# A local attention's band mask: from products on TensorE to one add-and-max on VectorE and selects on GpSimd

## Chip, cores, metric

The kernel runs on one core of a Trainium2 chip. The metric is its device time in microseconds (us), the median of several executions.

## The reference

Two decoder layers for 16 batch entries of 256 tokens and 256 features, all in fp32. The change is in the second block of the first layer, a cross attention in a local window:

```python
q, k, v = heads(x @ Wq + bq), heads(ctx @ Wk + bk), heads(ctx @ Wv + bv)   # 16 heads of 16 features
scores = einsum("bhqd,bhkd->bhqk", q, k) / sqrt(16)
scores = where(abs(i - j) <= 64, scores, masked)                           # a band: 64 keys to each side
x = layernorm(x + softmax(scores) @ v @ Wo + bo)
```

Around it stand a linear attention with a feed-forward network, a chain of six attention cells ("c" below, full 256 by 256 scores), a causal linear attention, a second cross attention with a padding mask ("y" below) and a Fourier layer. They are not changed.

## The kernel before

Every entry goes through the same list of some 500 steps. A step is a short piece of work on one engine: a product, a transposition, an eviction of a PSUM bank, a reduction. Four entries are under way at a time, each with its own buffers, and a fifth starts when the first is done. `program_plan` runs over all steps of all entries with a cost in us for each, as written in `entry_steps` (`do(engine, op, a, us, needs...)`), and picks for every engine, whenever it is free, a ready step, by entry and by the length of what hangs on it, with a little noise from `SEEDS`. What comes out are fixed lists, `PLAN["PE"]`, `PLAN["DVE"]`, `PLAN["ACT"]`, `PLAN["POOL"]` and `PLAN["SP"]`: each engine works through its own list in order and waits on semaphores where something is not there yet. So a step that takes longer than its cost says holds up what stands behind it on its engine, whatever the entry. PSUM has eight banks, and the plan assigns them too.

The attention works on quads: eight heads go in one step, four groups of 32 partitions with two heads in each, one of the two zeroed in the keys. The local attention has four such steps per entry, n = 0 to 3, kind "x", hence 64 in the kernel. One of them goes like this:

- `s` on TensorE (`tensor`, op "s"): the scores, queries on the partitions, four banks, each with two runs of 192 columns (`SPAN`), since a block of 128 queries sees at most 192 keys. Before, `banded` first writes the band into each bank (a product of `ident_bf` with `band`, 2 x 192 columns of 0 or -1e30 in bf16), and the score products add to it.
- `s` on VectorE, once for each pair p of banks: the maxima over the keys, negated, into `nmx`.
- `split` on VectorE: the maxima as three bf16 parts. `nm` on TensorE transposes them, and ScalarE copies them into SBUF.
- `st` on TensorE: the same scores again, transposed (keys on the partitions). Before, `banded` comes first here too; then the score products, and a product of `ones_bf` with the negated maxima that subtracts them.
- `exp` on ScalarE, for each pair p: exponentials from PSUM to `work` in SBUF, two banks of 2 x 192 columns each.
- `pv` on TensorE: the exponentials times the values. The row sums come with it, then `part`, `sums` and `norm`.

The quads of kinds "c" and "y" go the same way with 256 columns and without a band. GpSimd's list holds mostly the elementwise products of the first attention ("mix1" and "mix2", 16 of each per entry, `L1631` and `L1641`).

Of the kernel before, what the change touches and what calls it, by code (L numbers as in the profile page):

```python
# [72 lines left out]
SEEDS = (981929, 264616, 376881, 660340, 622402, 125658, 701981, 998496, 712956, 113630)  # L73
# [73 lines left out]
def entry_steps():  # L147
# [59 lines left out]
    def heads(n, q, k, v):  # L207
        kind, c, f, par = quad(n)
        b = do("PE", "s", n, 0.88 if kind != "x" else 1.4, q, k, *((nm_done[n - 2],) if n >= 2 else ()),
               takes=("score", "score"))  # L210
        maxed = [do("DVE", "s", (n, p), 1.13 if kind != "x" else 0.87, b, frees=((b, p),)) for p in range(2)]
# [4 lines left out]
        s = st_done[n] = do("PE", "st", n, 1.12 if kind != "x" else 1.6, nm,   # L216
# [3 lines left out]
        both = (do("DVE", "add", n, 1.2, *e),) if kind == "c" else ()  # L220
        pv = do("PE", "pv", n, 1.3 if kind == "c" else 0.9, *e, *both, v,
# [245 lines left out]
class Dry:  # L467
# [7 lines left out]
    affine_select = dma_start = stream_shuffle = wait_ge = then_inc = drain = _self  # L475
# [9 lines left out]
def build(nc, x, ctx_in, mask, w_all, w_setup, cols, rows, ew, act_w, out):  # L485
    ctx = ExitStack()
    with ctx:
# [22 lines left out]
        ones_bf = sb("ones_bf", [P, P], BF16)  # L510
        ewb = sb("ewb", [P, 3 * NODES])
# [178 lines left out]
        def tensor(e):  # L690
# [61 lines left out]
            def banded(b, count):  # L752
                for j in range(count):
                    e.matmul(b[j // 2][j % 2].rearrange("p (c n) -> p c n", c=NC)[:, :, 0:SPAN], ident_bf[:, :],  # L754
                             band[:, :, :], start=True, stop=False)

# [10 lines left out]
            for i, op, a, units in PLAN["PE"]:  # L767
# [106 lines left out]
                elif op == "s":  # L874
# [12 lines left out]
                    if kind == "x":  # L887
                        banded(b, 4)
                    for cc in range(NC):
                        kk = queries(kind, cc)  # L890
                        for g in range(4):
                            ins = e.matmul(b[g // 2][g % 2][:, cc * 256:cc * 256 + kk.stop - kk.start],  # L892
                                           q[32 * g:32 * g + 32, f, cc * P:cc * P + P],
                                           k[32 * g:32 * g + 32, f, kk], start=(kind != "x"),
                                           stop=(kind != "x" or cc == NC - 1), tile_position=(32 * g, 0))
# [9 lines left out]
                elif op == "st":  # L905
# [4 lines left out]
                    if kind == "x":  # L910
                        banded(b, 4)
                    e.wait_ge(*when("nm", a, i))
                    for kc in range(NC):
                        qq = queries(kind, kc)
                        o = slice(kc * 256, kc * 256 + qq.stop - qq.start)
                        for g in range(4):
                            e.matmul(b[g // 2][g % 2][:, o], k[32 * g:32 * g + 32, f, kc * P:kc * P + P],  # L917
                                     q[32 * g:32 * g + 32, f, qq], start=(kind != "x"), stop=False,
                                     tile_position=(32 * g, 0))
                        for g in range(4):  # L920
                            ins = e.matmul(b[g // 2][g % 2][:, o], ones_bf[32 * g:32 * g + 3, :],  # L921
# [892 lines left out]
```

## Time and profile before

| | |
|---|---|
| median of 3 runs | 3567.08 us (3566.13 to 3568.82) |
| profiled execution, own time | 3568.07 us |
| its span | 3566.3 us |
| granted TensorE clock, mean | 0.964 of full speed |
| TensorE busy | 3242.3 us, 91% |
| VectorE busy | 2329.9 us, 65% |
| ScalarE busy | 1695.1 us, 48% |
| GpSimd busy | 1019.1 us, 29% |

The span is the stretch from the first to the last instruction that the profiler recorded; the time of the execution is 1.8 us longer. Busy is the union of an engine's instructions, so time in which two of them overlap counts once.

### The profile page before, as it was taken

The numbers are of one execution on the slowest core, as the hardware profiler recorded it, in microseconds if no ns is written. First come the engines' busy times: TensorE is split into PE (matmuls) and PEld (weight loads), VectorE is DVE, ScalarE is ACT, GpSimd is POOL, SyncE is SP. The second block draws the span as 40 slices with busy tenths as digits, with TensorE's granted clock in tenths as the row PEclk, the third lists the DMA queues.
The fourth block names the chain that finished last, engine by engine and source line by source line (L and its number), as shares of the span: only waits on it lengthen the run. The fifth ranks groups of instructions, "written<-read, shape, count | busy, mean of one in ns | idle before, by whom it ended". The sixth has DMA issues, their size and how long they took to land.

```text
span 3566.3 us, 77500 instructions
## 1 busy us (share of the span) xinstructions
PE 3242.3 (91%) x31372; PEld 2395.2 (67%) x31372; DVE 2329.9 (65%) x4137; ACT 1695.1 (48%) x3472; POOL 1019.1 (29%) x795
## 2 busy tenths in 40 slices
PE   7899999998999999899999999999899999999876
PEld 6777767676766667676666766667676666766644
DVE  6675658667676766767577675766767676464533
ACT  1244454544545455444635445354454545554532
POOL 7872006042331413333041332304233141000000
PEclk8999999999999999999999999999999999999986
DMA  6210011010101101010100101101010110100000
GB/s 207 89 45 31 19 29 39 29 40 19 46 19 40 31 23 46 16 41 26 37 28 25 43 19 37 31 29 39 19 46 19 40 31 16 37 14 10 13 7 4
DMA packets 123276, 122.88 MB, mean 34 GB/s; under 512 B 9776, under 2 KB 122672, under 8 KB 122800
## 3 DMA queue, kind: packets, MB, share of 16 engines
q1 hardware_dynamic: 122928, 117.91, 10.9%
q8 instruction: 258, 4.23, 0.5%
q14 instruction: 90, 0.74, 0.1%
HBM read 113.69 MB, written 4.19 MB: 33 GB/s over the span
## 4 chain that ended last, share of the span: by engine, by line
PE 60%; DVE 15%; ACT 9%; issue 8%; POOL 7%; DMA 1%; SPq 0%; DVEq 0%; POOLq 0%; ACTq 0%
PE banks L747 16%; PE banks L739 11%; PE banks L892 7%; PE banks L917 6%; DVE nmx L1251 5%; PE banks L945 5%; POOL work L1641 3%; ACT work L1482 3%; PE banks L732 2%; PE banks L754 2%; PE banks L855 2%; PE banks L903 2%; POOL work L1631 2%; PE banks L952 1%; PE banks L921 1%
## 5 line engine op out<-in xcount | busy, mean ns | idle before, releaser
L747 PE MATMUL banks<-work,weights 128*128 128x256 f32 x3584 | 868.3, 390 | 56.4 <-DVE work L1275 51.5
L1251 DVE TENSOR_REDUCE nmx<-banks 128x4 f32<-128x1024 f32 (+3 forms) x684 | 725.4, 1099 | 250.5 <-PE banks L892 248.7
L747 PEld LDWEIGHTS banks<-work,weights 128*128 128x128 f32 x3584 | 678.3, 194 | 189.0 <-DVE work L1275 53.9
L1482 ACT ACTIVATE work<-banks 128x1024 f32<-128x1024 f32 (+3 forms) x679 | 595.1, 937 | 288.7 <-PE banks L921 288.7
L739 PE MATMUL banks<-weights,work 128*128 128x256 f32 x2688 | 653.7, 389 | 20.7 <-ACT work L1482 4.4
L739 PEld LDWEIGHTS banks<-weights,work 128*128 128x128 f32 x2688 | 499.3, 193 | 124.9 <-issue 39.7
L1641 POOL TENSOR_TENSOR work<-work 128x512 f32<-128x512 f32 x256 | 407.3, 1615 | 366.4 <-DVE work L1221 216.9
L892 PE MATMUL banks<-work 32*128 32x256 f32 (+1 forms) x5120 | 357.5, 394 | 60.5 <-DVE nmx L1251 27.2
L917 PE MATMUL banks<-work 32*128 32x256 f32 (+1 forms) x5120 | 391.4, 394 | 18.0 <-DVE nmx L1251 6.8
L1631 POOL TENSOR_TENSOR work<-work 128x512 f32<-128x512 f32 x256 | 346.6, 1375 | 148.7 <-DVE work L1217 134.7
L1269 DVE TENSOR_TENSOR added<-work 128x1024 f32<-128x1024 f32 x192 | 281.3, 1469 | 129.3 <-ACT work L1482 118.7
L945 PE MATMUL banks<-work 128*32 128x256 f32 (+3 forms) x5632 | 341.2, 364 | 5.3 <-ACT work L1482 4.6
L1675 POOL TENSOR_TENSOR work<-work,row 128x512 f32<-128x512 f32 x64 | 91.9, 1437 | 888.0 <-PE banks L732 888.0
L892 PEld LDWEIGHTS banks<-work 32*128 32x128 f32 x5120 | 234.6, 187 | 157.2 <-issue 125.7
L917 PEld LDWEIGHTS banks<-work 32*128 32x128 f32 x5120 | 214.0, 190 | 132.1 <-issue 81.2
L945 PEld LDWEIGHTS banks<-work 128*32 128x32 f32 x5632 | 158.3, 111 | 148.4 <-issue 82.4
L1384 ACT ACTIVATE work<-banks,cb 128x256 f32<-128x256 f32 x384 | 161.4, 475 | 149.2 <-PE banks L747 149.2
L1221 DVE TENSOR_REDUCE work<-work 128x32 f32<-128x512 f32 x256 | 173.2, 678 | 86.2 <-POOL work L1641 85.7
L1466 ACT ACTIVATE work<-banks 128x256 f32<-128x256 f32 x320 | 119.2, 385 | 212.7 <-PE banks L903 212.3
L1217 DVE TENSOR_REDUCE work<-work 128x32 f32<-128x512 f32 x256 | 171.6, 679 | 69.7 <-POOL work L1631 68.1
L921 PE MATMUL banks<-work,ones_bf 3*128 3x256 bf16 (+1 forms) x2560 | 190.8, 272 | 0.0
L732 PE MATMUL banks<-ident,work 128*128 128x128 f32 x768 | 122.1, 285 | 67.0 <-DVE work L1201 47.6
(156 smaller groups left out, 3525.2 us busy)
## 6 DMA issues: line engine op xcount, KB each, us to landing
weights<-in_w_all SPq DMA_DIRECT2D x322, 256.0 KB, 2.8
work<-in_w_setup SPq DMA_DIRECT2D x41, 256.0 KB, 5.1
work<-in_ctx SPq DMA_DIRECT2D x32, 256.0 KB, 3.1
work<-in_x SPq DMA_DIRECT2D x16, 256.0 KB, 3.0
out<-work SPq DMA_DIRECT2D x16, 256.0 KB, 2.2
weights<-in_w_all SPq DMA_DIRECT2D x1, 3072.0 KB, 15.0
row<-in_rows SPq DMA_DIRECT2D x1, 1280.0 KB, 9.2
mrow<-in_mask SPq DMA_DIRECT2D x16, 32.0 KB, 3.2
```

The costliest lines, as they stand in the source:

```text
L732: ins = e.transpose(b[:, f * 256 + c * P:f * 256 + c * P + P], src[:, c, f * P:f * P + P], ident[:, :])
L739: ins = e.matmul(b[:, m * 256:m * 256 + 256], xin[:, k, m * P:m * P + P], wslot(w)[:, k, :], start=(k == 0 and (m == 0 or closed)) if star ...
L747: ins = e.matmul(b[:, m * 256:m * 256 + 256], wslot(w)[:, k, m * P:m * P + P], xin[:, k, :], start=(k == 0 and (m == 0 or closed)) if star ...
L892: ins = e.matmul(b[g // 2][g % 2][:, cc * 256:cc * 256 + kk.stop - kk.start], q[32 * g:32 * g + 32, f, cc * P:cc * P + P], k[32 * g:32 * g ...
L917: e.matmul(b[g // 2][g % 2][:, o], k[32 * g:32 * g + 32, f, kc * P:kc * P + P], q[32 * g:32 * g + 32, f, qq], start=(kind != "x"), stop=False,
L921: ins = e.matmul(b[g // 2][g % 2][:, o], ones_bf[32 * g:32 * g + 3, :], upper(stored_nmax(s, a))[32 * g:32 * g + 3, qq], start=False, stop ...
L945: ins = e.matmul(b[32 * g:32 * g + 32, lo:hi], left, right[:, kc * 256 + lo - qq.start:kc * 256 + hi - qq.start], start=(kc == 0), stop=(k ...
L1251: ins = e.tensor_reduce(nmax(s, n)[:, 2 * p + j:2 * p + end, :], b.rearrange("p j (c n) -> p j c n", c=NC)[:, :, :, 0:w], AX, ALU.max, neg ...
L1269: e.tensor_tensor(added[:, half], pt(half, 0, 4)[:, :, 0:S], pt(half, 0, 4)[:, :, S:2 * S], ALU.add).then_inc(*tell(vec[s], "added", a, i))
L1482: ins = e.activation(dst, b.rearrange("p j (c n) -> p j c n", c=NC)[:, :, :, 0:w], ACT.Exp)
L1631: e.tensor_tensor(big1, q.unsqueeze(2).broadcast_to([P, PH, NH, DH]), k.unsqueeze(1).broadcast_to([P, PH, NH, DH]), ALU.mult).then_inc(*te ...
L1641: e.tensor_tensor(big2, mix.unsqueeze(2).broadcast_to([P, PH, DH, NH]), v.unsqueeze(1).broadcast_to([P, PH, DH, NH]), ALU.mult).then_inc(* ...
```

## The change

In the local attention the band leaves TensorE. `banded` is gone from `s` and `st`. The maxima are taken by four VectorE instructions for each pair of banks, one for each bank and block of queries: each adds the band to 192 columns of scores in PSUM, writes the sum back there, and gives the maximum of the sums as its accumulator output. These maxima are not negated, so `st` subtracts them with a constant of -1 (`minus_bf`). The transposed scores have no band any more; ScalarE takes exponentials of all 192 columns, and a new GpSimd step, `band`, then sets those outside the band to zero with four selects for each pair. `pv` waits for it. The plan's costs and its `SEEDS` are changed as well, so all the lists are made anew.

```diff
-SEEDS = (981929, 264616, 376881, 660340, 622402, 125658, 701981, 998496, 712956, 113630)
+SEEDS = (271952, 450768, 66414, 843758, 204716)
...
-        b = do("PE", "s", n, 0.88 if kind != "x" else 1.4, q, k, *((nm_done[n - 2],) if n >= 2 else ()),
+        b = do("PE", "s", n, 0.88, q, k, *((nm_done[n - 2],) if n >= 2 else ()),
                takes=("score", "score"))
-        maxed = [do("DVE", "s", (n, p), 1.13 if kind != "x" else 0.87, b, frees=((b, p),)) for p in range(2)]
+        maxed = [do("DVE", "s", (n, p), 1.13, b, frees=((b, p),)) for p in range(2)]
...
-        s = st_done[n] = do("PE", "st", n, 1.12 if kind != "x" else 1.6, nm, 
+        s = st_done[n] = do("PE", "st", n, 1.12 if kind != "x" else 1.0, nm, 
...
+        if kind == "x":
+            e = [do("POOL", "band", (n, p), 1.0, e[p]) for p in range(2)]
         pv = do("PE", "pv", n, 1.3 if kind == "c" else 0.9, *e, *both, v,
...
-            def banded(b, count):
-                for j in range(count):
-                    e.matmul(b[j // 2][j % 2].rearrange("p (c n) -> p c n", c=NC)[:, :, 0:SPAN], ident_bf[:, :],
-                             band[:, :, :], start=True, stop=False)
...
                     b = [take("score", "max", a, 0, i), take("score", "max", a, 1, i)]
-                    if kind == "x":
-                        banded(b, 4)
...
                     book(i, a)
-                    if kind == "x":
-                        banded(b, 4)
                     e.wait_ge(*when("nm", a, i))
+                    added_row = minus_bf if kind == "x" else ones_bf
...
+                        if kind == "x" and kc == 0:
+                            e.wait_ge(*when("band", a, 0, i))
+                            e.wait_ge(*when("band", a, 1, i))
...
                     w = SPAN if kind == "x" else S
+                    if kind == "x":
+                        for j in range(2):
+                            b = at("max", n, p, i)[j]
+                            for c in range(NC):
+                                ins = e.tensor_tensor_reduce(out=b[:, c * 256:c * 256 + SPAN], in0=b[:, c * 256:c * 256 + SPAN], in1=band[:, c, :],
+                                                             scale=1.0, scalar=3 * MASKED, op0=ALU.add, op1=ALU.max,
+                                                             accum_out=small[s]["nmx"][:, n % 2, c, 32 * (2 * p + j):32 * (2 * p + j) + 1])
+                        ins.then_inc(*freed("max", n, p, i))
+                        continue
...
+                elif op == "band":
+                    n, p = a
+                    e.wait_ge(*when("exp", n, p, i))
+                    both = pt(half_of.get((i, n), 0), 2 * p, 2)
+                    for lo, hi, base, sign in ((0, WINDOW, WINDOW, 1), (WINDOW, SPAN, 0, -1), (256, 256 + P, 0, 1),
+                                               (256 + P, 256 + SPAN, 0, -1)):
+                        part = both[:, :, lo:hi]
+                        ins = e.affine_select(out=part, in_=part, compare_op=ALU.is_ge, fill=0.0, base=base,
+                                              pattern=[[0, 2], [sign, hi - lo]], channel_multiplier=-sign)
+                    ins.then_inc(*tell(pool[s], "band", n, p, i))
```

TensorE's list, in the middle of the program, at a place where a quad of the local attention is scored (`s`) and the first one of the same entry is exponentiated (`st`). Before, each row of score products (`L892`, `L917`) has the four band products (`L754`) ahead of it:

```order
L754 MATMUL banks<-band,ident_bf 128x2x192 x4
L892 MATMUL banks<-work 128x192 x8
L739 MATMUL banks<-weights,work 128x256 x4
L747 MATMUL banks<-work,weights 128x256 x4
L903 MATMUL banks<-ident,nmx 128x128 x2
L754 MATMUL banks<-band,ident_bf 128x2x192 x4
L917 MATMUL banks<-work 128x192 x4
L921 MATMUL banks<-work,ones_bf 128x192 x4
```

Now, at the corresponding place (`L888` scores, `L898` the transposition of the maxima, `L911` and `L915` the transposed scores and the subtraction, `L942` the products with the values, all other rows products and transpositions of other steps):

```order
L888 MATMUL banks<-work 128x192 x8
L742 MATMUL banks<-weights,work 128x256 x4
L735 MATMUL banks<-ident,work 128x128 x4
L750 MATMUL banks<-work,weights 128x256 x4
L911 MATMUL banks<-work 128x192 x4
L915 MATMUL banks<-work,minus_bf 128x192 x4
L911 MATMUL banks<-work 128x192 x4
L915 MATMUL banks<-work,minus_bf 128x192 x4
L888 MATMUL banks<-work 128x256 x8
L750 MATMUL banks<-work,weights 128x256 x4
L888 MATMUL banks<-work 128x256 x8
L898 MATMUL banks<-ident,nmx 128x128 x4
```

The band products are gone. Behind the last of these rows comes the `pv` of the same quad, so 4 rows of other work (two of scores, one of four products, one of four transpositions) stand between `st` and `pv`.

VectorE's list. Before, the maxima of the first quads of an entry in the local attention (`L1251`) and their split (`L1257`, `L1260`):

```order
L1251 TENSOR_REDUCE nmx<-banks 128x2x2
L1257 TENSOR_TENSOR nmx<-nmx 128x4x2
L1260 TENSOR_TENSOR nmx<-nmx 128x4x2
L1251 TENSOR_REDUCE nmx<-banks 128x2 x2
L1221 TENSOR_REDUCE work<-work 128x32
```

Now, the last of the eight pairs of rows that one quad has, and what comes behind:

```order
L1251 ISA banks,nmx<-banks,band 128x192
L1251 ISA nmx 128x1
L1341 TENSOR_TENSOR work<-work,banks 128x512
L1363 SCALAR_TENSOR_TENSOR work<-banks,ykw,work 128x512 x2
L1175 BN_STATS st<-work 128x6 x2
L1179 BN_AGGR mv<-st 128x2 x2
L1263 TENSOR_TENSOR nmx<-nmx 128x4x2
L1266 TENSOR_TENSOR nmx<-nmx 128x4x2
```

Where one row took the maxima of two banks, eight rows stand now: for each bank and block of queries the add-and-max, and behind it a second instruction that writes out the accumulator.

GpSimd's list, where the next entry's products `mix1` (`L1638`) go on; the selects are `L1658`:

```order
L1629 TENSOR_SCALAR work<-work 128x512 x2
L1638 TENSOR_TENSOR work<-work 128x512 x8
L1658 AFFINE_SELECT work<-work 128x2x64
L1658 AFFINE_SELECT work<-work 128x2x128 x2
L1658 AFFINE_SELECT work<-work 128x2x64 x2
L1658 AFFINE_SELECT work<-work 128x2x128 x2
L1658 AFFINE_SELECT work<-work 128x2x64
L1638 TENSOR_TENSOR work<-work 128x512 x2
```

Eight selects for a quad are new, inside the run of products; before, that run was not interrupted by the local attention. Of the four quads of this entry two stand in this run, and two in a quieter stretch ahead of it.

## Rows read from the trace of the kernel before

**Rows 1.** The page's first part: busy time of each engine.

```profile
PE 3242.3 (91%) x31372; PEld 2395.2 (67%) x31372; DVE 2329.9 (65%) x4137; ACT 1695.1 (48%) x3472; POOL 1019.1 (29%) x795
```

**Rows 2.** The chain that ended last: shares by engine, shares by line.

```profile
PE 60%; DVE 15%; ACT 9%; issue 8%; POOL 7%; DMA 1%; SPq 0%; DVEq 0%; POOLq 0%; ACTq 0%
...
by line: PE banks L747 16.2%; PE banks L739 11.3%; issue 8.3%; PE banks L892 6.6%; PE banks L917 5.8%; DVE nmx L1251 5.4%; PE banks L945 4.8%; POOL work L1641 3.4%; ACT work L1482 3.2%; PE banks L732 2.2%; PE banks L754 2.1%; PE banks L855
```

**Rows 3.** One entry's period in mid-run: stretch, length, busy (instructions), clock.

```profile
1637.00:1849.00 212.00, 196.10 (x1945) 144.03 (x1938) 146.01 (x256) 105.41 (x217) 63.42 (x48) 0.98 0.11 32
```

**Rows 4.** Groups by form, PE: busy us, mean ns; idle before, releasers.

```profile
L754 PE MATMUL banks<-band,ident_bf 128*128 128x384 bf16 x512 | 111.1, 342 | 16.7 <-DVE nmx L1251 13.4 <-ACT work L1482 1.6 <-DVE work L1287 1.1
```

**Rows 5.** Timeline of PE, an `st` and an `s`: start us, us, line.

```profile
1732.08 0.81 PE L754 MATMUL banks<-band,ident_bf 128*128 128x384 bf16 x4 [1.10 <-DVE nmx L1251]
1732.82 0.61 PE L917 MATMUL banks<-work 32*128 32x192 f32 x8
...
1748.33 0.82 PE L754 MATMUL banks<-band,ident_bf 128*128 128x384 bf16 x4
1749.08 0.93 PE L892 MATMUL banks<-work 32*128 32x192 f32 x16
```

**Rows 6.** The page's group of L1251, then DVE groups by form.

```profile
L1251 DVE TENSOR_REDUCE nmx<-banks 128x4 f32<-128x1024 f32 (+3 forms) x684 | 725.4, 1099 | 250.5 <-PE banks L892 248.7
...
L1251 DVE TENSOR_REDUCE nmx<-banks 128x4 f32<-128x768 f32 x114 | 105.2, 949 | 33.0 <-PE banks L892 32.7
L1275 DVE TENSOR_TENSOR work<-banks,work 128x256 f32<-128x256 f32 x192 | 80.5, 419 | 116.6 <-ACT work L1497 116.3
L1329 DVE TENSOR_TENSOR work<-banks,causal 128x512 f32<-128x512 f32 x128 | 78.2, 678 | 3.8 <-PE banks L1024 3.8
L1285 DVE SCALAR_TENSOR_TENSOR work<-banks,em,work 128x256 f32<-128x256 f32 x64 | 30.8, 481 | 231.6 <-PE banks L945 231.6
L1170 DVE RECIPROCAL kept<-kept 128x1 f32<-128x1 f32 x16 | 2.6, 164 | 0.6
```

**Rows 7.** Timeline of DVE: start to start of back-to-back instructions.

```profile
1660.42 0.96 DVE L1251 TENSOR_REDUCE nmx<-banks 128x4 f32<-128x768 f32 x1 [1.97 <-PE banks L892]
1661.29 0.17 DVE L1257 TENSOR_TENSOR nmx<-nmx 128x8 f32<-128x8 f32 x1
...
1745.49 0.25 DVE L1182 BATCH_NORM_AGGREGATE mv<-st 128x2 f32<-128x6 f32 x2
```

**Rows 8.** Timeline of POOL: the selects that build the constants.

```profile
4.33 0.30 POOL L1581 TENSOR_SCALAR_AFFINE_SELECT ident<-ident 128x128 f32<-128x128 f32 x1 [0.23 <-POOL eps L1578]
4.58 0.30 POOL L1581 TENSOR_SCALAR_AFFINE_SELECT ident_bf<-ident_bf 128x128 bf16<-128x128 bf16 x1
...
5.11 0.52 POOL L1586 TENSOR_SCALAR_AFFINE_SELECT band<-band 128x384 bf16<-128x384 bf16 x1
5.58 0.29 POOL L1588 TENSOR_SCALAR_AFFINE_SELECT causal<-causal 128x128 bf16<-128x128 bf16 x1
```

**Rows 9.** Two DVE lines (min/median/max ns), and a stretch with GpSimd beside.

```profile
L1269 DVE TENSOR_TENSOR added<-work x192: 1210/1226/2286, 233.9 to 3463.2; 128x1024 f32<-128x1024 f32 x192
L1275 DVE TENSOR_TENSOR work<-banks,work x192: 391/423/426, 239.1 to 3468.7; 128x256 f32<-128x256 f32 x192
...
1740.37 1.27 POOL L1675 TENSOR_TENSOR work<-work,row 128x512 f32<-128x512 f32 x1 [28.43 <-PE banks L732]
1740.52 2.20 DVE L1269 TENSOR_TENSOR added<-work 128x1024 f32<-128x1024 f32 x1 [1.26 <-ACT work L1482]
```

**Rows 10.** Who waited for whom: us in total, times, longest us.

```profile
PEld banks L903 <- DVE nmx L1260: 42.2, 22, 4.6
PE banks L903 <- DVE nmx L1260: 35.7, 16, 4.2
```

**Rows 11.** Timeline behind that `st`: its exponentials, the next `pv`.

```profile
1733.98 1.57 ACT L1482 ACTIVATE work<-banks 128x768 f32<-128x768 f32 x3 [2.27 <-PE banks L921]
...
1736.25 0.90 PE L945 MATMUL banks<-work 128*32 128x192 f32 x24
```

More of the change, by code:

```diff
@@ L474 @@
     scalar_tensor_tensor = tensor_reduce = reciprocal = tensor_copy = bn_stats = bn_aggr = memset = _self
-    affine_select = dma_start = stream_shuffle = wait_ge = then_inc = drain = _self
+    tensor_tensor_reduce = affine_select = dma_start = stream_shuffle = wait_ge = then_inc = drain = _self
 class Signal:
@@ L510, in build @@
         ones_bf = sb("ones_bf", [P, P], BF16)
+        minus_bf = sb("minus_bf", [P, P], BF16)
         ewb = sb("ewb", [P, 3 * NODES])
@@ L893, in tensor @@
                                            q[32 * g:32 * g + 32, f, cc * P:cc * P + P],
-                                           k[32 * g:32 * g + 32, f, kk], start=(kind != "x"),
-                                           stop=(kind != "x" or cc == NC - 1), tile_position=(32 * g, 0))
+                                           k[32 * g:32 * g + 32, f, kk], start=True, stop=True, tile_position=(32 * g, 0))
                             if cc == NC - 1 and g == 1:
@@ L917, in tensor @@
                             e.matmul(b[g // 2][g % 2][:, o], k[32 * g:32 * g + 32, f, kc * P:kc * P + P],
-                                     q[32 * g:32 * g + 32, f, qq], start=(kind != "x"), stop=False,
+                                     q[32 * g:32 * g + 32, f, qq], start=True, stop=False,
                                      tile_position=(32 * g, 0))
                         for g in range(4):
-                            ins = e.matmul(b[g // 2][g % 2][:, o], ones_bf[32 * g:32 * g + 3, :],
+                            ins = e.matmul(b[g // 2][g % 2][:, o], added_row[32 * g:32 * g + 3, :],
                                            upper(stored_nmax(s, a))[32 * g:32 * g + 3, qq], start=False,
-                                           stop=(kind != "x" or kc == NC - 1), tile_position=(32 * g, 0))
+                                           stop=True, tile_position=(32 * g, 0))
                             if kc == NC - 1 and g == 1:
@@ L1571, in gpsimd @@
             e.memset(ones_bf[:, :], 1.0)
+            e.memset(minus_bf[:, :], -1.0)
             e.memset(mark[:, :, :], 0.0)
```

## The prediction

> **What bounds the kernel now.** I read the page's first part, then the chain, then one period in mid-run, then the places where the change works. TensorE is busy 91% of the span, VectorE 65%, GpSimd 29% [rows 1]. A stretch of 212 us in mid-run, one entry's period, says the same: TensorE 196.1 us, VectorE 146.0, GpSimd 63.4, at a granted clock of 0.98 [rows 3]. The chain that ended last lies 60% on TensorE, 15% on VectorE, 7% on GpSimd [rows 2]. So TensorE is the bound, but not alone: 9% of the span (324 us) it has nothing running, and the longest waits that I name below are for VectorE. Four entries interleave, and each engine's list is fixed. So an edit counts by how much of it lies on that chain, and I use the chain's shares as exchange rates.
>
> **What it takes off TensorE.** 64 quads have a set of four band products ahead of `s` and another ahead of `st`: 512 products, 128 sets. Together they are busy 111.1 us [rows 4]. The start of a set to the start of the score products behind it is 1749.08 - 1748.33 = 0.75 us for an `s` and 0.74 for an `st` [rows 5]; the set reads 0.82 busy because its end overlaps what follows. So 128 x 0.75 = 96 us of issue time go, and that is the most that this part can give. Of these products 2.1% of the span, 75 us, lies on the chain [rows 2]; with the overlap taken out, 75 x 0.75 / 0.82 = 68 us. I take -68. The score products and the subtraction keep their counts and columns: 0.
>
> **What it puts on VectorE.** A pair of banks had one reduction over 768 columns, 949 ns long, the next instruction starting 0.87 us after it [rows 6, 7]. Where the two banks are not neighbours it was split in two. 128 pairs now have four add-and-max instructions of 192 columns and four that write out the accumulator. Neither stands in the trace. The first reads PSUM and one tensor in SBUF, as two lines do that take 419 ns for 256 columns and 678 for 512: 1.01 ns a column, so 354 ns for 192 [rows 6]. Instructions that follow each other start about 0.08 us before the last one ends (0.949 against 0.87), so 0.27 from start to start. The second instruction writes one column; two tiny ones in a row take 0.25 us together, each some 0.15 to 0.17 long, so about 0.10 from start to start [rows 6, 7]. Lower bound of a couple: 0.27 + 0.07 (a start 0.08 ahead of the end of the shortest) = 0.34. Upper bound: neither overlaps, 0.354 + 0.164 = 0.52, and 0.06 more if it decodes like the line with a per-partition scalar, which takes 481 where the plain one takes 419 [rows 6]: 0.58. I take 0.40: all the operands are constants, and every VectorE row that I looked at overlaps its successor, with something added because the second needs the first's sum. So 4 x 0.40 = 1.60 for a pair instead of 0.87, and 128 x 0.73 = 94 us more on VectorE. Of line L1251's 725 us, all attentions together [rows 6], the chain holds 5.4% of the span, 193 us, or 27% [rows 2]; 0.27 x 94 = +25.
>
> The plan reckons 1.13 us for such a pair, less than my 1.60, so behind each pair the VectorE list runs 0.5 us late against the plan. What stands there is the split, which TensorE's transposition of the maxima waits for (42.2 and 35.7 us in total before) [rows 10], and other entries' evictions. The 27% covers this as long as the lateness is a few us a quad.
>
> **What it puts on GpSimd.** Two selects of 128 columns start 0.25 us apart, one of 384 is followed after 0.47 [rows 8]: 0.86 ns a column and 0.14 fixed. A pair has two selects of 2 x 64 and two of 2 x 128 columns: 2 x 0.25 + 2 x 0.36 = 1.22 us. These were bf16 or fp32 constants, and the new ones are fp32 with two levels; the nearest rows for the other end are GpSimd's ordinary operations (1.27 us for 512 columns) [rows 9], 2.5 ns a column, which would make it 768 x 2.5 = 1.9 us. 128 x 1.22 = 156 us on 1019, 33% of the span. What hides it: in the list of TensorE four rows of other work stand between an `st` and its `pv`, 44 instructions as the trace counts them, at the period's pace (196.1 / 1945 = 0.10 us) 4.4 us. Needed are the exponentials, which take 1.57 us for both pairs [rows 11], the first pair done after some 0.8, then 2 x 1.22: 3.3 us. So it fits by 1 us at that place, and if GpSimd is in the middle of a product of 1.3 us it just doesn't. Inside the run of products `mix1` the selects wait for the exponentials, and the products behind them wait too; those belong to an entry that has just begun. I take +4.
>
> With the selects comes some contention. The add with two inputs in SBUF takes 1226 ns in the median and up to 2286; the row that took 2.20 us began 0.15 us after GpSimd began one of 1.27, and ended about one normal duration after GpSimd did. The line with one input in PSUM never exceeds 426 ns [rows 9]. The new add-and-max is of the second sort, so GpSimd doesn't hold it. The selects can hold the first sort, for at most 0.25 to 0.36 us, 4% of the time: within the +4. The Trainium skill, *SBUF — State Buffer*, Who interferes with whom, says that a VectorE instruction with two SBUF inputs shares an interface with GpSimd's reads and the later one is blocked; the trace agrees.
>
> **The sum.** From the profiled execution's own time, 3568: -68 + 25 + 4 = -39, so 3529, and with the order new everywhere no finer than 3530. The profiled execution is 1 us above the median of the runs, so no correction. 0.2% is 7 us, about what a measurement of this kernel can tell from no change.
>
> **Rivals.**
>
> - *The gain in full* (0.14). The new VectorE work falls into its idle 35%, and only issue time on TensorE counts: 3568 - 96 = 3472, to 3505 with a third of it lost. For it: the period has 66 us of VectorE idle per entry and needs 6 more. Against it: VectorE already stands on 15% of the chain, and `s`, maxima, split, `nm` and `st` of a quad are one chain.
> - *The add-and-max is dear, and VectorE takes over in the local attention* (0.23); this one ends on the other side. At 0.58 a pair takes 2.32, 186 us more than before. A quad then holds VectorE 4.6 us in a piece, against the 2.3 that the plan reckons, and all other entries' evictions, transposed maxima and layer norms wait behind it. The part above my 94 us, 92 us, then counts nearly in full: 3529 + 92 = 3621 at the most, 3590 with two thirds. It decides from the price at which the excess eats the 39 us: at the full rate 39 / 512 = 0.08 above 0.40, so slower from about 0.48 us a couple. The Trainium skill has a rule for this case: *VectorE: DVE Perf Modes*, The DRAIN you can't avoid, says that the next operation does not start until the pipe is empty, and another section of that page that an accumulator output makes two instructions. The order shows the two instructions; the starts 0.08 us ahead of the end speak against the first rule. What it would give here, worked out from the durations: 0.354 + 0.164 = 0.52 a couple, 61 us above my sum at the full rate, 3590, and 3545 at the 27%.
> - *GpSimd comes late* (0.07). At 1.9 us a pair, `pv` needs 0.8 + 3.8 = 4.6 us where 4.4 are covered, and 2 to 3 us where the selects wait behind a product or the products behind them. With 1 us for each of 64 `pv` it is 3529 + 64 = 3593. Against it: all selects in the trace are cheap, and GpSimd is idle two thirds of the time.
> - *The freed time turns into waits* (0.10). TensorE reaches every wait earlier, and what it waits for is no sooner there; the new order has its own idle spots among the 324 us. 3560 to 3575.
>
> The forecast itself has 0.46, with its own range 3505 to 3560: -39 with the couple at 0.34 (128 x 4 x 0.06 x 0.27 = 8 less) or 0.46 (up to 30 more), and an order that is luckier or unluckier by some 15 us.
>
> **How the numbers follow.** Faster: the forecast, the full gain, and the milder parts of the others (0.04): 0.64. Within 0.2%: most of the fourth and a little of the dear case: 0.13. Slower: 0.23. The range takes in the lower part of the full gain and the dear case up to two thirds of its excess: 3480 to 3600.
>
> **What the profile would show.** Right: line L754's 512 products gone, TensorE's busy time down by some 100 us to 3140; add-and-max rows of about 350 ns, at 192 columns, each couple 0.40 from start to start; VectorE's busy time up by 90 to 100 us; selects of 0.3 to 0.45 us each; waits for the maxima and the split (L1251 and their successors) up by some 25 us; waits of `pv` for the selects of a few us in all. Wrong, if the couples are 0.5 us or more apart and TensorE's waits for L1251 or for the split double; if `pv` waits for GpSimd for tens of us; or if TensorE's idle time grows by as much as its busy time fell.

## Result, and the profile after

| | before | after |
|---|---|---|
| median (4 runs each, same chip) | 3566.61 us (3562.03 to 3568.82) | 3474.55 us (3470.35 to 3488.09) |
| ratio, 95% interval | | 0.975 (0.972 to 0.978) |
| profiled execution: span | 3566.3 us | 3468.6 us |
| TensorE busy; span without it | 3242.3; 324.0 us | 3157.1; 311.5 us |
| granted TensorE clock, mean | 0.964 | 0.967 |

The change makes the kernel 92 us (2.5%) faster. Forecast were 3530 us, with a range of 3480 to 3600: the sign is right, the time lies 55 us below the forecast and 5 below the range.

The first and the fourth part of the page after (busy times, chain):

```profile
PE 3157.1 (91%) x30860; PEld 2362.2 (68%) x30860; DVE 2319.2 (67%) x5004; ACT 1695.7 (49%) x3492; POOL 1202.3 (35%) x1308
...
PE 60%; DVE 16%; POOL 9%; issue 7%; ACT 6%; DMA 1%; SPq 1%; POOLq 0%; DVEq 0%; ACTq 0%
```

Against [rows 1, 2]: TensorE has 512 instructions and 85 us less, its idle time fell by 12 too. GpSimd has 513 instructions and 183 us more. VectorE has 867 instructions more and yet 11 us less busy time.

The times of the changed kernel scatter more than those of before, and its interval of 0.3% is some 11 us to either side. It stands behind every difference to the changed kernel below.

Where in the span does the time come from? The timeline of SyncE has one store for each of the 16 entries of the batch. Before, the third one, two in mid-run, and the last:

```profile
900.63 0.38 SPq L1750 DMA_DIRECT2D out<-work  x1
...
1535.51 0.38 SPq L1750 DMA_DIRECT2D out<-work  x1
1747.10 0.38 SPq L1750 DMA_DIRECT2D out<-work  x1
...
3563.73 0.38 SPq L1750 DMA_DIRECT2D out<-work  x1
```

After, the same stores:

```profile
901.73 0.38 SPq L1767 DMA_DIRECT2D out<-work  x1
...
1510.08 0.38 SPq L1767 DMA_DIRECT2D out<-work  x1
1714.13 0.38 SPq L1767 DMA_DIRECT2D out<-work  x1
...
3465.99 0.38 SPq L1767 DMA_DIRECT2D out<-work  x1
```

Up to the third store nothing is gained (900.6 and 901.7). The time comes from the 13 intervals behind it: 2663.1 us before, 2564.3 after, 7.6 us an interval. In mid-run an entry took 211.6 us, and now some 204 and 202. Two such periods after (columns as in [rows 3]):

```profile
1510.00:1714.00 204.00, 191.92 (x1906) 142.91 (x1905) 142.99 (x310) 105.28 (x219) 74.74 (x79) 0.97 0.11 32
1714.00:1916.00 202.00, 190.24 (x1906) 142.01 (x1905) 143.30 (x310) 105.51 (x220) 74.74 (x80) 0.98 0.11 33
```

TensorE's busy time in a period fell from 196.1 [rows 3] to 191.1, its idle time from 15.9 to 11.9. So a period gains 5 us of work and 4 us of waits. The clock is nearly the same (0.98 before, 0.97 and 0.98 now).

The add-and-max in VectorE's timeline, one quad:

```profile
1664.31 0.42 DVE L1281 TENSOR_TENSOR work<-banks,work 128x256 f32<-128x256 f32 x1
1664.65 0.35 DVE L1251 CUSTOM_DVE_ANT_0 banks<-banks,band 128x192 f32<-128x192 f32 x1
1664.92 0.14 DVE L1251 DVE_READ_ACCUMULATOR2_ANT nmx<- 128x1 f32 x1
1664.92 0.40 DVE L1251 CUSTOM_DVE_ANT_0 banks<-banks,band 128x192 f32<-128x192 f32 x1
1665.24 0.14 DVE L1251 DVE_READ_ACCUMULATOR2_ANT nmx<- 128x1 f32 x1
1665.24 0.40 DVE L1251 CUSTOM_DVE_ANT_0 banks<-banks,band 128x192 f32<-128x192 f32 x1
...
1667.13 0.14 DVE L1251 DVE_READ_ACCUMULATOR2_ANT nmx<- 128x1 f32 x1
1667.38 0.17 DVE L1263 TENSOR_TENSOR nmx<-nmx 128x8 f32<-128x8 f32 x1
```

Each read of the accumulator starts in the same moment as the next add-and-max, where one stands behind it. The couples are 0.315 us apart (1664.92, 1665.24, ...), a pair of banks takes 1.26 instead of 0.87, and all 128 pairs take 50 us more, not 94.

Forms of VectorE and of GpSimd after (columns as in [rows 4]):

```profile
L1275 DVE TENSOR_TENSOR added<-work 128x1024 f32<-128x1024 f32 x192 | 272.2, 1423 | 116.3 <-ACT work L1488 98.0 <-issue 16.0 <-PE banks L915 0.8
L1251 DVE CUSTOM_DVE_ANT_0 banks<-banks,band 128x192 f32<-128x192 f32 x512 | 164.9, 393 | 19.9 <-PE banks L888 19.6
L1198 DVE TENSOR_SCALAR work<-work,mv,rstd 128x256 f32<-128x256 f32 x256 | 97.7, 428 | 26.5 <-ACT rstd L1399 26.5
L1266 DVE TENSOR_TENSOR nmx<-nmx 128x8 f32<-128x8 f32 x320 | 73.2, 229 | 11.3 <-DVE nmx L1263 0.4
L1251 DVE DVE_READ_ACCUMULATOR2_ANT nmx<- 128x1 f32 x512 | 73.0, 143 | 0.0
```

```profile
L1658 POOL TENSOR_SCALAR_AFFINE_SELECT work<-work 128x256 f32<-128x256 f32 x256 | 99.0, 413 | 0.0
L1658 POOL TENSOR_SCALAR_AFFINE_SELECT work<-work 128x128 f32<-128x128 f32 x256 | 73.1, 299 | 285.6 <-ACT work L1488 285.6
```

The same three old forms before:

```profile
L1269 DVE TENSOR_TENSOR added<-work 128x1024 f32<-128x1024 f32 x192 | 281.3, 1469 | 129.3 <-ACT work L1482 118.7 <-issue 9.1
L1201 DVE TENSOR_SCALAR work<-work,mv,rstd 128x256 f32<-128x256 f32 x256 | 119.3, 508 | 33.0 <-ACT rstd L1393 32.7
L1260 DVE TENSOR_TENSOR nmx<-nmx 128x8 f32<-128x8 f32 x320 | 111.6, 349 | 10.9
```

The three do the same work in 443.1 us instead of 512.2. That is 69 us, and it hides the add-and-max in VectorE's sum. The reason can be seen in the timeline of before: a tiny VectorE instruction beside a product of GpSimd, started 0.04 us after it, takes as long as the product, where 0.17 us is its own time:

```profile
1803.99 1.27 POOL L1631 TENSOR_TENSOR work<-work 128x512 f32<-128x512 f32 x1 [1.81 <-DVE work L1217]
1804.03 1.26 DVE L1260 TENSOR_TENSOR nmx<-nmx 128x8 f32<-128x8 f32 x1
```

How often the two meet is a matter of the order. Of the 320 instructions of this line 51 take over 1.2 times the median in the trace of before, and 17 after. Before's own work on the lists of the changed kernel (an experiment below) has 16, and a mean of 228 ns where after has 229:

```profile
L1262 DVE TENSOR_TENSOR nmx<-nmx 128x8 f32<-128x8 f32 x320 | 72.8, 228 | 11.2 <-DVE nmx L1259 0.2
```

TensorE's own waits after:

```profile
PE banks L888 <- ACT work L1390: 37.6, 35, 2.3
PE banks L735 <- DVE work L1198: 29.0, 7, 14.1
PE banks L898 <- DVE nmx L1266: 27.9, 21, 4.5
```

Before, the longest one was of other work (51.5 us for the evictions of L1275), and those for the split were 35.7 [rows 10].

### The profile page after: what moved, and what is told of

Read it like the earlier page. It is cut to its first block, busy times and chain, and to the rows that moved or that the text cites. A ratio compares the mean times of both kernels' runs of the same rounds, so it can differ in the third digit from the quotient of the medians.

```text
span 3468.6 us, 77951 instructions
## 1 busy us (share of the span) xinstructions
PE 3157.1 (91%) x30860; PEld 2362.2 (68%) x30860; DVE 2319.2 (67%) x5004; ACT 1695.7 (49%) x3492; POOL 1202.3 (35%) x1308
## 4 chain that ended last, share of the span: by engine, by line
PE 60%; DVE 16%; POOL 9%; issue 7%; ACT 6%; DMA 1%; SPq 1%; POOLq 0%; DVEq 0%; ACTq 0%
PE banks L750 17%; PE banks L742 13%; PE banks L888 7%; DVE nmx L1257 6%; PE banks L911 5%; PE banks L942 4%; POOL work L1648 4%; POOL work L1638 4%; ACT work L1488 3%; PE banks L1021 2%; PE banks L735 2%; PE banks L853 2%; DVE work L1218 2%; PE banks L898 1%; PE banks L949 1%
## 5 line engine op out<-in xcount | busy, mean ns | idle before, releaser
L750 PEld LDWEIGHTS banks<-work,weights 128*128 128x128 f32 x3584 | 667.6, 192 | 161.3 <-issue 51.0
L1257 DVE TENSOR_REDUCE nmx<-banks 128x4 f32<-128x1024 f32 (+1 forms) x527 | 605.0, 1188 | 209.7 <-PE banks L888 209.3
L1488 ACT ACTIVATE work<-banks 128x1024 f32<-128x1024 f32 (+2 forms) x699 | 595.7, 913 | 281.5 <-PE banks L915 279.2
L911 PE MATMUL banks<-work 32*128 32x256 f32 (+1 forms) x5120 | 395.2, 395 | 39.7 <-DVE nmx L1257 15.4
L888 PE MATMUL banks<-work 32*128 32x256 f32 (+1 forms) x5120 | 359.9, 396 | 67.1 <-ACT work L1390 37.6
L1638 POOL TENSOR_TENSOR work<-work 128x512 f32<-128x512 f32 x256 | 346.8, 1380 | 51.1 <-DVE work L1209 28.6
L1692 POOL TENSOR_TENSOR work<-work,row 128x512 f32<-128x512 f32 x64 | 107.6, 1681 | 731.0 <-PE banks L735 731.0
L942 PE MATMUL banks<-work 128*32 128x256 f32 (+3 forms) x5632 | 331.5, 356 | 25.2 <-DVE nmx L1257 16.6
L1275 DVE TENSOR_TENSOR added<-work 128x1024 f32<-128x1024 f32 x192 | 272.2, 1423 | 116.3 <-ACT work L1488 98.0
L888 PEld LDWEIGHTS banks<-work 32*128 32x128 f32 x5120 | 239.5, 189 | 152.8 <-issue 102.6
L911 PEld LDWEIGHTS banks<-work 32*128 32x128 f32 x5120 | 216.1, 190 | 173.5 <-issue 88.8
L942 PEld LDWEIGHTS banks<-work 128*32 128x32 f32 x5632 | 153.6, 109 | 164.2 <-issue 83.9
L1658 POOL TENSOR_SCALAR_AFFINE_SELECT work<-work 128x128 f32<-128x128 f32 (+1 forms) x512 | 158.6, 356 | 285.6 <-ACT work L1488 285.6
L1251 DVE CUSTOM_DVE_ANT_0 banks<-banks,band 128x192 f32<-128x192 f32 x512 | 164.9, 393 | 19.9 <-PE banks L888 19.6
```

Source lines behind the costliest of these rows:

```text
L750: ins = e.matmul(b[:, m * 256:m * 256 + 256], wslot(w)[:, k, m * P:m * P + P], xin[:, k, :], start=(k == 0 and (m == 0 or closed)) if star ...
L942: ins = e.matmul(b[32 * g:32 * g + 32, lo:hi], left, right[:, kc * 256 + lo - qq.start:kc * 256 + hi - qq.start], start=(kc == 0), stop=(k ...
L1257: ins = e.tensor_reduce(nmax(s, n)[:, 2 * p + j:2 * p + end, :], b.rearrange("p j (c n) -> p j c n", c=NC)[:, :, :, 0:w], AX, ALU.max, neg ...
L1275: e.tensor_tensor(added[:, half], pt(half, 0, 4)[:, :, 0:S], pt(half, 0, 4)[:, :, S:2 * S], ALU.add).then_inc(*tell(vec[s], "added", a, i))
L1488: ins = e.activation(dst, b.rearrange("p j (c n) -> p j c n", c=NC)[:, :, :, 0:w], ACT.Exp)
L1638: e.tensor_tensor(big1, q.unsqueeze(2).broadcast_to([P, PH, NH, DH]), k.unsqueeze(1).broadcast_to([P, PH, NH, DH]), ALU.mult).then_inc(*te ...
```

## The experiments

Every ratio is to the kernel before, run on the same chip, with its 95% interval. The profiled execution's TensorE idle time (span without busy time) stands beside it.

### The parts one by one

**The kernel before without band products** (lists and reductions untouched).

```diff
-                    if kind == "x":
-                        banded(b, 4)
```

> The kernel before with its lists as they are, and only the 512 band products left out (so the local attention has no mask). It prices what TensorE is freed of, with the old order and the old maxima. By my recorded term: 68 us less than before, 3499. By the rival that all issue time of TensorE counts (0.75 us for each of 128 sets): 96 less, 3471. If the freed time turns into waits: under 30 less, above 3537.

Measured: 3531.15 us, 0.990 (0.9885 to 0.9915), 34 us less than before's 3565.16 in the same job. Its busy times:

```profile
PE 3165.3 (90%) x30860; PEld 2363.0 (67%) x30860; DVE 2330.7 (66%) x4137; ACT 1695.4 (48%) x3472; POOL 1019.4 (29%) x795
```

TensorE's busy time fell by 77 us and its idle time rose from 324.0 to 363.1. So half of what was taken off came back as waits. My 68 for this part is twice what it gives in the old order.

**The changed kernel with the band products put back** as dead work ahead of the score products, in both places.

> The changed kernel with its lists as they are, and the 512 band products put back ahead of the same score products, as dead work (what they write is overwritten). If the gain is TensorE's issue time and nothing else, the time goes from 3475 back up by 96, to 3570, that is, to the kernel before within 0.2%. If it only goes up by 68 or less, to 3543 or below, some 25 us or more of the gain come from the new order or from less contention.

Measured: 3520.46 us, 0.9864 (0.9848 to 0.9881); idle 280.3. The products are worth 46 us in the new order.

**The changed kernel without the selects** and without the waits for them.

```diff
                 elif op == "band":
+                    continue
```

> The changed kernel with its lists, without the 512 selects on GpSimd and without the wait for them (so the exponentials outside the band are not zeroed). By my recorded term of +4 us for GpSimd: 3470. If the selects are hidden wholly: 3475, the same within 0.2%. If the products of the first attention queue behind them and this counts: 20 us or more less, 3455.

Measured: 3456.4 us, 0.9694 (0.9679 to 0.9708); idle 291.5. The selects cost 18 us. Two ways are possible: `pv` waits for them, or they hold up other work. The page's list of those who waited for L1658 has `PE banks L942: 0.8, 2` (us, times) and speaks against the first. But it puts each wait down to one engine, and here to the wrong one. The products of `pv` over 192 columns stand in the local attention alone. In the changed kernel, without the selects, and with the band products put back:

```profile
L942 PE MATMUL banks<-work 128*32 128x192 f32 x512 | 34.1, 337 | 17.5 <-DVE nmx L1257 16.6 <-POOL work L1658 0.8
L939 PE MATMUL banks<-work 128*32 128x192 f32 x512 | 34.1, 338 | 0.0
L951 PE MATMUL banks<-work 128*32 128x192 f32 x512 | 34.1, 337 | 2.6 <-POOL work L1667 0.8 <-issue 0.6
```

TensorE stands still for 17.5 us just ahead of them, nearly all of the 18. One of the 13 waits that are put down to L1257:

```profile
1752.87 2.48 POOL L1658 TENSOR_SCALAR_AFFINE_SELECT work<-work 128x128 f32<-128x128 f32 x8
1754.34 2.36 DVE L1257 TENSOR_REDUCE nmx<-banks 128x4 f32<-128x1024 f32 x2 [0.70 <-PE banks L888]
1755.56 0.54 PEld L942 LDWEIGHTS banks<-work 128*32 128x32 f32 x16 [1.66 <-DVE nmx L1257]
1755.59 0.67 PE L942 MATMUL banks<-work 128*32 128x192 f32 x12 [1.28 <-DVE nmx L1257]
```

The last select of the quad ends 0.25 us ahead of `pv`, and in 11 of the 13 cases this distance is 0.25 us. The first reduction of L1257 ends at 1755.57, when the weights of `pv` are already being loaded; so it is in 11 of the 13. It is the selects, then, that `pv` waits for, 1.3 us for one of the four quads in 13 of the 16 entries. Here the exponentials had ended at 1751.89, but GpSimd was in a product (L1638) that ended at 1752.92. Little is left for the other way: of the 77 VectorE instructions that start while a select runs, one takes over 0.01 us more than the median of its line (0.32 for 0.18 us).

**The changed kernel with plain reductions.** One reduction for each pair, over all 192 columns without the band; the selects stay.

```diff
                     if kind == "x":
+                        for j, end, b in spans("max", n, p, i):
+                            ins = e.tensor_reduce(nmax(s, n)[:, 2 * p + j:2 * p + end, :],
+                                                  b.rearrange("p j (c n) -> p j c n", c=NC)[:, :, :, 0:w], AX, ALU.max)
+                        ins.then_inc(*freed("max", n, p, i))
+                        continue
```

> The changed kernel with its lists, and one reduction for each pair of banks again in place of four add-and-max instructions with their accumulator reads (maxima over all 192 columns, without the band). The trace has a couple at 0.32 us from start to start, 1.27 us a pair against 0.87: 51 us of VectorE time. At the 27% that I reckoned: 14 us less, 3461. If this work falls into VectorE's idle time: the same as the changed kernel, 3475 within 0.2%. At the full rate: 3424.

Measured: 3468.21 us, 0.9727 (0.9713 to 0.9742); idle 302.2. The add-and-max costs 6 us here, which the interval of the changed kernel does not tell from nothing.

**The changed kernel with 138 us of VectorE work more.** A reduction over the same 192 columns ahead of each add-and-max, its result unused.

```diff
                             for c in range(NC):
+                                k = 8 * n + 4 * p + 2 * j + c
+                                e.tensor_reduce(spare[:, s, k:k + 1], b[:, c * 256:c * 256 + SPAN], AX, ALU.max)
+                            for c in range(NC):
```

> The changed kernel with its lists and four more reductions of 192 columns for each pair of banks of the local attention (their results go nowhere), 0.27 us each from start to start: 138 us more on VectorE, as if an add-and-max with its read took 0.59 us instead of 0.32. At the 27% that I reckoned: 37 us more, 3512. At the full rate, which my rival put on such a price: 3475 + 138 = 3613, the kernel slower than before. By the rate that the run with the old reductions showed (6 us for 51, 12%): 3491.

Measured: 3541.52 us, 0.9937 (0.992 to 0.9955), 67 us above the changed kernel; idle 365.6. The added form:

```profile
L1253 DVE TENSOR_REDUCE spare<-banks 128x1 f32<-128x192 f32 x512 | 157.4, 348 | 17.7 <-PE banks L889 17.7
```

So VectorE time in this place counts at 67 / 138 = 49% when it is much. Had the couples taken 0.58 us, the change would have been at about this point (an estimate: the added reductions start 0.27 us apart by their length, and 0.315 + 0.27 is 0.585).

### The order

**Before's work on the lists of the changed kernel.** The plan gets after's costs, steps and `SEEDS`; GpSimd passes over the select steps.

```diff
-SEEDS = (981929, 264616, 376881, 660340, 622402, 125658, 701981, 998496, 712956, 113630)
+SEEDS = (271952, 450768, 66414, 843758, 204716)
...
+                elif op == "band":
+                    continue
```

> The work of the kernel before (band products, old reductions, no selects) on the lists of the changed kernel; its list entries for the selects are passed over. Theory now: the lists themselves bring most of the gain. The runs so far put the band products at +46 on these lists, the selects at -18 without them, the add-and-max at -6 without it, so 3475 + 46 - 18 - 6 = 3497, 70 less than before with the same work. Rival: the three parts hide each other, and together they come to the kernel before, 3555 or more.

Measured: 3519.19 us, 0.9879 (0.9857 to 0.9901), against 3564.81 in the same job. The same work, in another order, takes 46 us less. (The banks are assigned anew too, so 27 VectorE instructions less and 20 ScalarE instructions more do it.) I had expected 3497 from the parts one by one; the time is 22 us above that. Its busy times:

```profile
PE 3239.4 (92%) x31372; PEld 2396.3 (68%) x31372; DVE 2271.4 (65%) x4110; ACT 1701.3 (48%) x3492; POOL 1046.2 (30%) x795
```

TensorE is as busy as before (3242.3), but idle for 271.2 us instead of 324.0. VectorE does the same work in 58 us less. This is the luck of the order, with none of the change in it. What in the order does it I did not take apart.

**Each kernel with the other's noise numbers** (`SEEDS` alone exchanged, every cost its own).

> The kernel before, work and costs as they are, with the other noise numbers (SEEDS) of the changed kernel. If the numbers are any draw as good as another, 3567 within 30. If each set was a lucky one for its own list of costs, a foreign set is worse by more: 3620 or above.

> The changed kernel with the noise numbers of before; work and costs as changed. Theory: the gain of the change is a lucky order more than less work, so this comes out well above 3475: 3530 or more. Rival: the order matters little and the gain stays, 3475 to 3490.

Measured: the kernel before 3675.28 us, 1.0314 (1.0294 to 1.0334); the changed one 3645.95, 1.0223 (1.0198 to 1.0248). Each is far slower with numbers that were not chosen for it, by 109 and 171 us. With after's numbers the change is worth 201 us, with before's it costs 81. Neither pair is evidence on the change.

**One noise number that nobody chose, for both kernels**: 0, 1, 2 and 3.

```diff
-SEEDS = (981929, 264616, 376881, 660340, 622402, 125658, 701981, 998496, 712956, 113630)
+SEEDS = (0,)
```

> The kernel before with one noise number, 0, in place of its ten: an order that nobody chose. By the swing that the foreign numbers gave (3565 to 3675), 3600 to 3750.

> The changed kernel with the same one noise number, 0. If the change as such is worth what its three parts add up to (-34 or -46 for the band products, +6 for the maxima, +18 for the selects: about 10 to 22 less), the median of such pairs lies there; one pair can lie 100 to either side. If it is worth much more in an order made for it, as the recorded rival had it, 60 to 100 less.

> The kernel before with one noise number, 1. As b_draw0, 3600 to 3750.

> The changed kernel with the noise number 1. As a_draw0: between 110 less and 90 more than b_draw1 if the parts say it all, 60 to 100 less on average if not.

> The kernel before with the noise number 2 for its order. Draws so far: 3626 and 3743 with numbers that nobody chose, and 3675 with the changed kernel's numbers. This one 3600 to 3750 us.

> The changed kernel with the noise number 2. Pairs of one number so far: +29 and -69 us for numbers that nobody chose, -201 and +81 for numbers chosen for one of the two. If the draw decides: anywhere from 110 less to 90 more than the kernel before with this number. If the change itself is worth its recorded 39 us or more, mostly below zero, around -40.

> The kernel before with the noise number 3 for its order: 3600 to 3750 us, as for number 2; it serves as the other half of a pair with one number.

> The changed kernel with the noise number 3: as for number 2, if the draw decides anywhere from 110 less to 90 more than the kernel before with this number; if the change itself is worth its recorded 39 us or more, below zero, around -40.

| number | before's work, us, ratio | changed work, us, ratio | difference |
|---|---|---|---|
| 0 | 3626.46, 1.0167 (1.0151 to 1.0182) | 3655.82, 1.0251 (1.0236 to 1.0266) | +29 |
| 1 | 3742.7, 1.0498 (1.0481 to 1.0516) | 3673.42, 1.0295 (1.0275 to 1.0316) | -69 |
| 2 | 3729.35, 1.0465 (1.0444 to 1.0486) | 3643.94, 1.0218 (1.0193 to 1.0243) | -85 |
| 3 | 3729.8, 1.0464 (1.0439 to 1.0488) | 3692.16, 1.0368 (1.0338 to 1.0399) | -38 |

The mean of the differences is -41 us. They scatter by 51 us, so four of them leave the mean uncertain by 51 / 2 x 3.2 = 81 us at 95%: it fits the forecast's 39, it fits 92, and it doesn't exclude nothing. What it does show is the size of the luck. Before's work spreads over 116 us in four orders, and the chosen order lies 141 us below their mean; the changed work has 48 and 192. The busy times with number 2, before and changed:

```profile
PE 3332.1 (89%) x31372; PEld 2434.7 (65%) x31372; DVE 2274.5 (61%) x4132; ACT 1704.5 (46%) x3495; POOL 1010.4 (27%) x795
```

```profile
PE 3211.9 (88%) x30860; PEld 2372.2 (65%) x30860; DVE 2328.7 (64%) x5025; ACT 1705.3 (47%) x3503; POOL 1179.6 (33%) x1308
```

With spans of 3729.4 and 3629.4 us, TensorE is idle for 397 and 418 us. Its busy time grows too, for the same instructions: by 90 us for before's work, where the granted clock is 0.944 instead of 0.964, and by 55 for the changed work (0.955 instead of 0.967). So in these two the order costs twice: for the gaps, and for a lower clock. The clock doesn't follow the gaps alone, though: with number 0 before's work has TensorE idle for 360 us at 0.970.

### A version of both

**The change with plain reductions, planned for it.** The four costs of a quad are set to what the traces show, and it has noise numbers of its own. The maximum over all 192 keys is at least that of the band, so it bounds the exponentials as well, and the softmax doesn't depend on what is subtracted, as long as no score outside the band is so much larger that the exponentials inside it vanish in fp32.

```diff
-        b = do("PE", "s", n, 0.88, q, k, *((nm_done[n - 2],) if n >= 2 else ()),
+        b = do("PE", "s", n, 0.88 if kind != "x" else 0.86, q, k, *((nm_done[n - 2],) if n >= 2 else ()),
...
-        maxed = [do("DVE", "s", (n, p), 1.13, b, frees=((b, p),)) for p in range(2)]
+        maxed = [do("DVE", "s", (n, p), 1.13 if kind != "x" else 0.87, b, frees=((b, p),)) for p in range(2)]
...
-        s = st_done[n] = do("PE", "st", n, 1.12 if kind != "x" else 1.0, nm, 
+        s = st_done[n] = do("PE", "st", n, 1.12 if kind != "x" else 1.06, nm, 
...
-            e = [do("POOL", "band", (n, p), 1.0, e[p]) for p in range(2)]
+            e = [do("POOL", "band", (n, p), 1.3, e[p]) for p in range(2)]
```

> The changed kernel with plain reductions over all 192 columns of a run in place of the add-and-max (a maximum taken over more keys than the band still bounds the exponentials, so the softmax is the same), with the plan's costs as the traces have them (0.87 for such a pair, 1.3 for a pair's selects, 0.86 and 1.06 for s and st), and with noise numbers of its own, picked for a short planned length. If a good order can be had for these costs as well, it is 6 us or more under the changed kernel: 3468 or below. If the changed kernel's order was just a lucky one on the chip: 3480 to 3530.

Measured: 3449.77 us, 0.9676 (0.9662 to 0.9689), 25 us below the changed kernel. Two periods of it:

```profile
1502.30:1705.10 202.80, 187.81 (x1912) 138.94 (x1908) 145.00 (x255) 105.49 (x218) 73.25 (x79) 1.00 0.11 33
1705.00:1907.50 202.50, 187.73 (x1912) 138.94 (x1908) 145.04 (x256) 105.50 (x218) 73.26 (x79) 1.00 0.11 33
```

TensorE gets by with 187.8 us in a period (191.1 in the changed kernel), at a clock of 1.00 instead of 0.97 to 0.98.

**The same lists with the add-and-max.**

> The same lists as c_plainmax, but with the add-and-max. Its extra 0.4 us for each pair isn't in the plan's costs here. By the 12% of the run with old reductions in the changed kernel's lists: 6 us above c_plainmax. By the 49% of the run with four more reductions: 25 above.

Measured: 3474.37 us, 0.9746 (0.973 to 0.9761). The add-and-max costs 25 us on these lists (6 on the others), 49% of its 50. This is also a second chosen order for the changed work, and it gives the time of the first, 3474.55.

## Why the prediction was wrong, point by point

- **The step that failed** is the last one of the forecast: "an order that is luckier or unluckier by some 15 us". Before's own work on after's lists gives 46 us (3564.8 to 3519.2), with nothing of the change in it. The rest of the measured 92, from 3519.2 to 3474.6, is 45 us: the change on fixed lists, for which the sum said 39. The four unchosen pairs, mean -41, say no different, with their wide interval. I took the order as a small error around the sum. It is larger than the sum, and the 15 us came from no row. The trace of before has a hint and no more: TensorE's 324 us of idle time had room.
- **That the sum of 39 lies so near the 45** is luck. On these lists the band products gave 22 us less than I took (46 for 68), and what add-and-max and selects cost together beside the band products was 28 less (1 for 29). The two errors nearly cancel.
- **Band products, -68**: they give 34 in the old order and 46 in the new. Their busy time was read well (85 us less at the end, and 77 without them, for the 100 forecast). What was mis-sized is the exchange: the chain's share said that 71% of 96 us count, and it was 35% to 48%. The chain names what ended last, and not how close behind it the next chain comes. This is what I had as a rival with 0.10 (freed time turns into waits); at half strength it is true.
- **The couple of 0.40 us**: it takes 0.315, below my lower bound of 0.34. The main instruction is longer than I had it (393 ns for 354), but the read of the accumulator costs no time of its own: 0.315 is the length of the main one, less the 0.08 by which every start comes early. The Trainium skill (*VectorE: DVE Perf Modes*, The DRAIN you can't avoid) says that the next operation waits for the pipe to empty, from which I had estimated 0.354 + 0.164 = 0.52; it adds, which the prediction left out, that a next operation that is not held starts earlier, and it is this that the rows above show.
- **The exchange of 27% on VectorE**: 12%, 49% and 49% in the three places where it was measured (6 of 50, 25 of 50, 67 of 138). The term of +25 came to +6 on after's lists, and +25 on the others.
- **Selects, +4**: each price was right (299 and 413 ns, a quad 2.46 us where 2 x 1.22 stood), but they cost 18. The prediction had the reason in a half sentence, that `pv` just has to wait when GpSimd is in the middle of a product, and it took 4 us for all of GpSimd. It happens for one quad in 13 of the 16 entries, 1.3 us each, and with a few smaller waits it comes to 17.5 us. That is a good part of the rival that GpSimd comes late, which had 0.07.
- **The terms don't add.** Taken out of the changed kernel one at a time they give -46 + 6 + 18 = -22, and together on fixed lists -45. With the band products in, add-and-max and selects cost 1 us together (3520.46 against 3519.19, give or take 10); without them 6 and 18, each taken out by itself. Of the 23 us between the two 15 are seen in the rows above: with the band products TensorE stands still ahead of this `pv` for 2.6 us instead of 17.5. So the selects hide under TensorE's fuller work; for the add-and-max that is not shown.
- **The gain in full** (3472 to 3505) names the measured time, but its mechanism is not what happened: it wants 96 us from the band products alone, and they give 34 to 46. **The dear add-and-max** fell by its price, 0.315 us.
- **What stays open**: how much of the 92 us is the change. Fixed lists say 45. Two chosen orders of the changed work meet at 3474, and two of before's stand at 3566 and 3519; whether a longer search would bring before's work lower still was not tried.

## What to carry to other kernels

Where a plan with noise fixes the order, a change of any cost draws a new order, and here that draw moves the time by more than the change: run the old work on the new lists first, and the new work with a part taken out, before giving a part the credit. A share of the chain is a poor exchange rate: for the band products it said 71% of their issue time where a third to a half came, and for VectorE 27% where 12% to 49% did. When an engine waits for several others, the profile names one of them: look at what ends a constant time ahead of it, and take the suspect out. And when a mask only keeps a maximum tight, try without it: a bound over more keys served as well here, and cost 25 us less on lists made for it and 6 (within the noise) on the others.

## What the hardware showed that I had not expected

- An accumulator read on VectorE (134 to 150 ns) starts in the same moment as the next instruction. 512 add-and-max of 192 columns from PSUM with their reads run at 0.315 us each.
- GpSimd holds a VectorE instruction with two inputs in SBUF for its whole length: one of 0.17 us took 1.26. The line of these (L1260) lost 349 - 176 = 173 ns on the mean of 320. L1201, with one tensor and two columns of scalars in SBUF, is held too: 36 that start beside a running GpSimd instruction take 1118 ns in the mean, the others 408. The add-and-max, with one input in PSUM, stays at 340 to 406 ns; 72 of the 512 start beside a running GpSimd instruction, and take 396 ns in the mean.
- The granted clock differs with the order: for before's work it was 0.944 to 0.970 as a mean over the span, the lowest in the order of number 2 (a span of 3729.4 us), the highest in that of number 0 (3619.3). The changed work had 0.934 (number 3) to 0.977 (the lists of the version of both).
